# Key pass of a linear attention beside a graph network: exponentials against normalised rows, Wv applied once per layer, turned rows kept in memory

## The chip, the cores and the metric

One core of a Trainium2 chip runs the whole program in one launch. The time is the device time of one execution in microseconds (us); the median of three executions is given, and one further execution was profiled.

## The reference

Per call there are 3125 nodes with 256 features, 100000 edges, and three parts whose results are summed and normalised:

```
xn = layernorm(x)
x  = x + gnn(xn, edge_attr, src, dst) + mix(xn)          # the two parts share nothing but xn
x  = x + moe(layernorm(x))                               # 16 experts, the best 2 for each row

mix, 4 layers, 8 heads of 32:
  h = layernorm(x) * g1 + b1
  q = softmax over each head of (h Wq) * s ; k = softmax over all 3125 rows of (h Wk) * s ; v = h Wv
  context = k^T v (per head) ;  x = x + (q context) Wo + bo
  x = x + gelu((layernorm(x) * g2 + b2) W1 + b1) W2 + b2  # 256 -> 1024 -> 256
gnn: relu([xn[src], attr] W1^T + b) summed by dst, then two products and a row norm
```

All products are in float32. The graph part has no work of a layer in it, and the kernel spreads its edge work over the four layers.

## The kernel before, in words

The 3125 rows are 25 tiles of 125 rows, in 5 groups (g) of 5 tiles. A layer (l) has three stages.

- **Key pass** (lines 1252 to 1285 on PE, 1675 to 1713 on DVE, 977 to 994 on ACT). For each group: keys are made transposed in four units (two of three tiles, two of two tiles; L1259), values in three units (`rows_at`, L1210, from `Wv_s`) that DVE copies to `V5` (L1697). DVE takes the running maximum (L1683) and the shift, ACT makes the exponentials `eT` (L983) and a correction `corr`. PE turns the normalised rows of the next group (`normalised_T`, L1220), ACT applies gain and shift (`features`, L910) into `TT`; PE turns `eT` (L1273), ACT copies it to `es` (L915), PE multiplies `es` with `V5`, 129 columns a head pair (the last column is ones and sums the exponentials; L1283), and DVE adds that to `ctxS` (L1711).
- **Middle** (L1287 to L1307): queries of group 0, the context turned and multiplied with Wo into `M_s` (L1299, L1730), attention of group 0 (`attention`), queries of group 1, the second norm of group 0.
- **Feed-forward pass** (L1310 to L1347), group by group: first product with W1 in 8 blocks f, each of 8 matmuls (L1319, ACT applies Gelu, L1015); then the turned rows and queries of group g+2, `queries_T` and `attention` of group g+1, and the second product of group g (`out_rows`, L1210). Groups 0 to 2 hold queries, groups 0 to 3 hold an attention.

Between these stand 224 edge steps (`step`, `pe_edges`, `act_edges`, `dve_edges`). A step is two bf16 products (L441, after the DMA of `aT`), on DVE `z` = product + gathered rows `G` (L481), on ACT `zr` (L449), on DVE the sum of the step before (L461), the one-hot matrix (L468) and `zl` (L455), and on PE in the next step eight products (L433, L434) that wait for `zl`. The tables `ST_K`, `ST_M`, `ST_P` say how many steps stand in each group: 2 or 3 in a key group, 4 in the middle, 8 or 7 in a feed-forward group.

Every engine runs its own list in the written order; the lists meet in semaphores. PSUM is used as two rings: `RING`, three banks that ACT frees (`ring`: unit u waits until u-3 is free), and `ROW`, two banks that DVE frees (`row_of`). SP issues the DMAs in one list: the `aT` loads, and at a layer's end the weights of the next (`weights_B`, 2.5 MB), which stand ahead of the next layer's first `aT`. GpSimd issues the gathers of `G`.

Of the kernel before, what the change touches and what calls it, by code (L numbers as in the profile page):

```python
# [11 lines left out]
def build(nc, x, src, dst, edge_attr, gnn_W1, gnn_b1, gnn_W2,  # L12
# [8 lines left out]
    T = 125  # L21
# [43 lines left out]
    zn_d = dram("zn_d", (N, D), f32)  # L65
    y_d = [dram(f"y{i}_d", (N + SL, D), f32) for i in range(2)]

    with ExitStack() as ctx:
# [47 lines left out]
        xT_all = over("xT", [128, 2, KD, 128], f32)  # L116
        xT_room = sb("xT_room", [128, 2 * KD * 128])
        QT = sb("QT", [128, KD, GT * T])
        V5 = sb("V5", [T, GT, KD, 129])
# [15 lines left out]
        ctxS = sb("ctxS", [128, KD, 129])  # L135
        ctxN = sb("ctxN", [128, KD, 128])
# [6 lines left out]
        corr = sb("corr", [128, 2, KD])  # L143
# [73 lines left out]
        V_rows = V5[:, :, :, :].rearrange("p j k n -> p (j k n)")[:, 0:GT * D].rearrange("p (j d) -> p j d", d=D)  # L217
# [52 lines left out]
        xs = [sb(f"xs{i}", [128, D])[:, :] for i in range(2)] + [TT[:, i, 0:D] for i in range(2)]  # L270
# [45 lines left out]
        cn_done, rk_done = sem("cn_done"), sem("rk_done")  # L316
# [27 lines left out]
        RING_GA = 4 + LNU + GT  # L344
# [3 lines left out]
        ROW_GA = NRP + 2  # L348
        RING_GP = [2 * NF + (LNU if g + 2 < NG else 0) + (GT + LNU if g + 1 < NG else 0) for g in range(NG)]
        ROW_GP = [NRP * (1 + (g + 1 < NG) + (g + 2 < NG)) for g in range(NG)]  # L350
        RING_MP, ROW_MP = 1 + LNU + GT + LNU, 3 * NRP + KD
        RING_A, RING_L = NT, LNU + NG * RING_GA + RING_MP + sum(RING_GP)
# [10 lines left out]
        HN_L = 3 * NT  # L363
# [4 lines left out]
        ST_K = [[2, 3 - l % 2, 3, 2, 2] for l in range(L)]  # L368
# [5 lines left out]
        def ring_k(l, g):  # L374
            return RING_A + l * RING_L + LNU + g * RING_GA

# [16 lines left out]
        def set_p(g):  # L393
            return 3 + NG + sum(1 + (n + 2 < NG) for n in range(g))

# [3 lines left out]
        def ring_q1(l, g):  # L399
            return ring_h1(l, NG) if g == 0 else ring_k(l, NG) + 1 if g == 1 else ring_p(l, g - 2) + 2 * NF  # L400

        def ring_qT(l, g):
            return ring_k(l, NG) + 1 + LNU if g == 0 else ring_p(l, g - 1) + 2 * NF + (LNU if g + 1 < NG else 0)
# [4 lines left out]
        def row_q(l, g):  # L408
            return row_k(l, NG) if g == 0 else row_k(l, NG) + 2 * NRP + KD if g == 1 else row_p(l, g - 2) + NRP

        def row_ao(l, g):
            return row_k(l, NG) + NRP + KD if g == 0 else row_p(l, g - 1)
# [1574 lines left out]
```

## Time and profile before

| | |
|---|---|
| time, median of 3 runs | 2347.33 us (2338.67, 2347.33, 2349.57) |
| time of the profiled execution | 2337.08 us, of which span 2335.3 us |
| PE busy | 1986.8 us (85%), weight loads 1637.1 us |
| DVE busy | 1520.7 us (65%) |
| ACT busy | 926.8 us (40%) |
| GpSimd busy | 1360.3 us (58%) |
| mean granted TensorE clock | 0.941 |

PE is TensorE, PEld its weight loads, DVE VectorE, ACT ScalarE, SP the engine that issues the DMAs. Busy time is the union of an engine's instructions. A matmul in float32 shows as two instructions, a transpose as one. The mean length of a matmul holds some 0.16 us that overlaps the next one, so the pace of a run of matmuls is read from the starts. In a timeline, an entry in square brackets is the idle time of the engine ahead of the row and what ended it.

### The profile page before, as it was taken

How to read it: one execution, taken by the hardware profiler on the slowest of the kernel's cores; microseconds unless marked ns; L12 is line 12 of the kernel's file. 1: busy time of each engine (PE TensorE's matmuls, PEld its weight loads, DVE VectorE, ACT ScalarE, POOL GpSimd, SP SyncE). 2: the span in 40 equal slices, each digit the busy share in tenths (PEclk: the TensorE clock that was granted, in tenths of full speed). 3: DMA queues.
4: the chain of work that ended last, by engine and by line, in shares of the span. 5: the costliest groups of instructions: out<-in, count | busy, mean ns of one | idle time of the engine just before them, and what ended most of it. 6: DMA issues, size and time to landing. Idle time of an engine off the chain costs nothing. (4 is left out here: it accounts for less than half of the span.)

```text
span 2335.3 us, 33082 instructions
## 1 busy us (share of the span) xinstructions
PE 1986.8 (85%) x10654; PEld 1637.1 (70%) x10654; DVE 1520.7 (65%) x3443; ACT 926.8 (40%) x1948; POOL 1360.3 (58%) x1123
## 2 busy tenths in 40 slices
PE   2449899999888999989899998989999885799990
PEld 1337677778776787877677777767777775788880
DVE  4748877776787777678777766887676457411116
ACT  1224444444445444344544443444444322233330
POOL 4156566677566666756666675656667500466650
PEclk7769999999999999999999999999999976899995
DMA  9553233233332233343232234233223521799997
GB/s 212 174 159 78 67 76 72 71 78 85 105 76 69 71 74 74 83 109 82 65 73 72 71 84 108 69 87 74 71 71 84 124 77 45 238 307 304 304 286 169
DMA packets 269780, 268.49 MB, mean 115 GB/s; under 512 B 146075, under 2 KB 203486, under 8 KB 269630
## 3 DMA queue, kind: packets, MB, share of 16 engines
q0 software_dynamic: 127488, 134.76, 24.2%
q1 hardware_dynamic: 138030, 131.85, 19.2%
q8 instruction: 75, 1.23, 0.2%
q10 hardware_dynamic: 4112, 0.03, 0.1%
q14 instruction: 75, 0.61, 0.1%
HBM read 230.37 MB, written 35.05 MB: 114 GB/s over the span
## 5 line engine op out<-in xcount | busy, mean ns | idle before, releaser
L846 POOL DMA_INDIRECT G<-P_d,src_T x896 | 1138.6, 1271 | 648.0 <-DVE z L481 383.9
L481 DVE TENSOR_TENSOR z<-bank,G 125x512 f32<-125x512 f32 x448 | 288.2, 685 | 167.4 <-PE bank L441 127.8
L1210 PE MATMUL bank<-W_s,hid 128*125 128x256 f32 x1600 | 363.2, 381 | 25.5 <-DVE qe L1621 25.5
L449 ACT ACTIVATE zr<-z 125x512 fp32r<-125x512 f32 x448 | 265.9, 627 | 293.7 <-DVE z L481 292.8
L455 DVE SCALAR_TENSOR_TENSOR zl<-z,zr 125x512 fp32r<-125x512 f32 x448 | 289.8, 688 | 131.1 <-ACT zr L449 131.1
L1319 PE MATMUL bank<-TT,W_s 128*128 128x250 f32 (+1 forms) x1280 | 356.1, 431 | 0.0
L1210 PEld LDWEIGHTS bank<-W_s,hid 128*125 128x125 f32 x1600 | 293.8, 188 | 71.7 <-issue 30.0
L1319 PEld LDWEIGHTS bank<-TT,W_s 128*128 128x128 f32 x1280 | 240.0, 192 | 95.3 <-issue 4.6
L433 PE MATMUL bank<-zr,onehot 125*125 125x256 f32 x896 | 267.6, 331 | 21.7 <-DVE zl L455 21.5
L1015 ACT ACTIVATE hid<-bank,b_s 128x375 f32<-128x375 f32 x320 | 166.1, 520 | 192.5 <-PE bank L1319 184.5
L434 PE MATMUL bank<-zl,onehot 125*125 125x256 f32 x896 | 226.8, 284 | 0.0
L433 PEld LDWEIGHTS bank<-zr,onehot 125*125 125x125 f32 x896 | 169.6, 189 | 46.1 <-DVE onehot L468 16.3
L910 ACT ACTIVATE TT<-bank,lnp 128x375 f32<-128x375 f32 x240 | 127.3, 614 | 143.1 <-PE bank L1220 142.1
L441 PE MATMUL bank<-Wst,aT 128*125 128x512 bf16 x448 | 138.1, 388 | 54.1 <-DMA aT<-attr_d 50.8
L434 PEld LDWEIGHTS bank<-zl,onehot 125*125 125x125 f32 x896 | 170.3, 190 | 5.9
L468 DVE TENSOR_TENSOR onehot<-iota_n,dst_T 125x500 fp32r<-125x500 f32 x224 | 154.2, 688 | 0.0
L1638 DVE TENSOR_TENSOR X<-bank,X 125x512 f32<-125x512 f32 (+1 forms) x120 | 70.6, 600 | 104.0 <-PE bank L1210 103.9
L1220 PE MATMUL bank<-ident,hn 125*128 125x125 f32 x600 | 95.7, 283 | 35.0 <-DVE hn L1561 14.0
L1084 ACT ACTIVATE QT<-bank,b1e 128x128 f32<-128x128 f32 x256 | 73.3, 370 | 98.6 <-PE bank L1435 98.6
L866 POOL DMA_INDIRECT xs<-zn_d,slot_tok x32 | 31.5, 983 | 138.0 <-DVE slot_tok L1915 121.4
L441 PEld LDWEIGHTS bank<-Wst,aT 128*125 128x125 bf16 x448 | 58.3, 138 | 74.1 <-issue 43.3
L1220 PEld LDWEIGHTS bank<-ident,hn 125*128 125x128 f32 x600 | 67.1, 142 | 61.2 <-ACT TT L910 23.9
(313 smaller groups left out, 3071.7 us busy)
## 6 DMA issues: line engine op xcount, KB each, us to landing
W_s<-in_L_ffn_w SPq DMA_DIRECT2D x64, 512.0 KB
hid<-in_L_ffn_w SPq DMA_DIRECT2D x64, 512.0 KB, 3.9
G<-P_d,src_T POOLq DMA_INDIRECT x896, 4.2
W_s<-in_L_mix_W SPq DMA_DIRECT2D x8, 1024.0 KB, 11.0
aT<-attr_d SPq DMA_DIRECT2D x224, 31.2 KB, 2.6
attr_d<-hn SPq DMA_DIRECT2D x12, 246.1 KB, 4.5
X<-in_x SPq DMA_DIRECT2D x5, 560.0 KB
P_d<-es SPq DMA_DIRECT2D x25, 112.0 KB
```

Source lines behind the costliest of these rows:

```text
L433: nc.tensor.matmul(sum_bank[0:T, 0:D], onehot[:, s, i, :], zr[:, s, i // 2, cols], start=i == 0, stop=False)
L434: ins = nc.tensor.matmul(sum_bank[0:T, 0:D], onehot[:, s, i, :], zl[:, i // 2, cols], start=False, stop=i == ST - 1)
L441: nc.tensor.matmul(edge_bank[k][0:ET, :], aT[:, s, :], Wst[:, 2 * k * D:2 * (k + 1) * D], start=True, stop=True).then_inc(e_done, 1)
L449: nc.scalar.activation(zr[:, s, k, :], z[:, k, :], ACT.Relu).then_inc(r_done, 1)
L455: nc.vector.scalar_tensor_tensor(zl[:, k, :], z[:, k, :], 0.0, zr[:, s, k, :].bitcast(f32), ALU.max, ALU.subtract).then_inc(lo_done, 1)
L468: nc.vector.tensor_tensor(onehot[:, s, :, :], iota_n[0:ET, :].unsqueeze(1).to_broadcast([ET, ST, T]), dst_T[:, ds(e * ST, ST)].unsqueeze(2 ...
L481: nc.vector.tensor_tensor(z[:, k, :], edge_bank[k][0:ET, :], G[:, ST * s + 2 * k:ST * s + 2 * k + 2, :].rearrange("p j d -> p (j d)"), ALU ...
L846: pool.indirect_dma_start(G[:, j, :], None, P_d[:, :], bass.IndirectOffsetOnAxis(ap=src_T[:, at:at + 1], axis=0)).then_inc(g_in[j], 16)
L1015: act.activation(hid[:, f, a * T:b * T], RING[(u - RING_A) % 3][:, 0:(b - a) * T], ACT.Gelu, bias=b1_s[:, l * NF + f:l * NF + f + 1]).then ...
L1210: ins = pe.matmul(to[0:T, (j - a) * D:(j - a) * D + D], w, m, start=n == 0, stop=n == len(pairs) - 1)
L1220: ins = pe.transpose(to[:, (j - a) * T:(j - a) * T + T], hn[:, j, 128 * k:128 * k + 128], ident[0:T, 0:T])
L1319: ins = pe.matmul(to[:, 0:(b - a) * T], W1_s[:, k, part], TT[:, k, TT_PIECES[pc]], start=k == 0, stop=k == KD - 1)
```

## The change

Five things are done, all in the layers.

1. The value product leaves the key pass. The exponentials are multiplied with the **normalised rows** (256 columns, without gain and shift), and the context becomes a 256x256 sum `ctxS`; the sum of exponentials comes from ACT's `accum_out` into `piece_sum` and is kept in `key_sum`. Once per layer `ctxS` is divided by `key_sum` (`ctxN`), turned (4 transposes), given gain and shift (`ctxF`), and multiplied with Wv (4 products, `ctxT`), and then with Wo.
2. This product (`context(g-1)`) is made **one group late**, between the third and the fourth key unit of group g; that of group 4 stands at the head of the middle. Rows and turned rows alternate between two buffers (`hn`/`hn2`, `TT`/`TTQ`).
3. The turned rows of each group are **kept in memory**: SP writes them to `nT_d` after the key pass's `features` (641 KB a group) and reads them back into `TTQ` for the queries, so the second turning of each group's first norm is gone.
4. Queries of groups 2, 3 and 4 are made **inside the first product** of the feed-forward of group g = 1, 2, 3 (`QIN`, after blocks 1, 3 and 5), for g+1, not for g+2 as before; ACT's exponential stands after block 6.
5. Edge steps are dealt out anew: `ST_K`, `FF_STEP` (steps after blocks 0, 2, 4, 6 in place of 0, 2, 5 and one behind the product); a third step of a key group stands behind the keys; a step stands in the middle of each attention; the first step of a key group's last two stands ahead of `normalised_T`.

```diff
-        ST_K = [[2, 3 - l % 2, 3, 2, 2] for l in range(L)]
+        ST_K = [[2 + l % 2, 2, 2, 2, 3] for l in range(L)]
-        FF_STEP = {0: 0, 2: 1, 5: 2}
+        FF_STEP, FF_Q = {0: 0, 2: 1, 4: 2, 6: 3}, {1: 0, 3: 1, 5: 2}
 # SP
+            def keep_normalised_T(l, g):
+                if g == 0:
+                    sp.wait_ge(nT_in, l * NG * 16)
+                sp.wait_ge(ring_act, ring_h1(l, g) + LNU + 1)
+                sp.dma_start(nT_d[g], NORM_T[g % 2][:, :, :].rearrange("p k n -> p (k n)")).then_inc(nT_out, 16)
+            def load_normalised_T(g):
+                sp.dma_start(TTQ_flat, nT_d[g]).then_inc(nT_in, 16)
             for l in range(L):
+                keep_normalised_T(l, 0)
+                at = step_k(l, 0) + (PG if l == 0 else 0)
+                for g in range(NG):
+                    attr_steps(at, step_k(l, g + 1))
+                    ...
 # ACT, key pass
                             act.activation(eT[:, h, a * T:b * T], RING[(u0 + 2 * pc + h - RING_A) % 3][:, 0:(b - a) * T], ACT.Exp,
-                                           bias=nb[:, pc, h:h + 1], scale=SCALE).then_inc(ring_act, 1)
+                                           bias=nb[:, pc, h:h + 1], scale=SCALE,
+                                           accum_out=piece_sum[:, g % 2, pc, h:h + 1]).then_inc(ring_act, 1)
-                        if pc == 0 and ST_K[l][g] == 3:
-                            step(step_k(l, g))
-                    first_norm(u0 + 4, u0 + 4 - RING_A)
+                    if ST_K[l][g] == 3:
+                        step(step_k(l, g))
+                    if g + 1 < NG:
+                        act.wait_ge(nT_out, (l * NG + g) * 16)
+                        first_norm(u0 + 4, u0 + 4 - RING_A, to=NORM_T[(g + 1) % 2])
 # ACT, middle
+                act.wait_ge(ring_full, uM + 1)
+                for k in range(KD):
+                    ins = act.activation(ctxF[:, k, :], ...)
+                ins.then_inc(ring_act, 1)
                 q_softmax(0)
-                copy_tile(uM, uM - RING_A, ctxT[:, :, :], 128)
-                first_norm(ring_q1(l, 1), ring_q1(l, 1) - RING_A)
                 step(eM)
                 queries_T(0)
 # ACT, feed-forward
                         if f - 1 in FF_STEP:
                             step(e0 + FF_STEP[f - 1])
+                        if QIN[g] and f == 6:
+                            q_softmax(g + 1)
 # PE, key pass
+                def context(g):
+                    r0, uT = row_k(l, g), ring_k(l, g + 1) - GT
+                    for pc, (a, b) in enumerate(PC):
+                        to = row_of(r0 + pc)
+                        for h in range(KD):
+                            for j in range(a, b):
+                                ...
+                                ins = pe.matmul(to[:, D * h:D * h + D], es[:, j, 128 * h:128 * h + 128], NORM[g % 2][:, j, :],
+                                                start=j == a, stop=j == b - 1)
+                        ins.then_inc(row_full, 1)
                     for pc, (a, b) in enumerate(PC):
                         for h in range(KD):
+                            if pc == 1 and h == 1 and g:
+                                context(g - 1)
                             to = ring(u0 + 2 * pc + h)
                             ...
-                        for i in ((0, 1), (2,))[pc]:
-                            rows_at(r0, i, lambda j: [(TT[:, k, tt_cols(j)], Wv_s[:, k, :]) for k in range(KD)])
-                    normalised_T(l * SETS + g + 1, u0 + 4)
+                    if ST_K[l][g] == 3:
+                        step(step_k(l, g))
                     step(step_k(l, g + 1) - 2)
+                    if g + 1 < NG:
+                        normalised_T(l * SETS + g + 1, u0 + 4, NORM[(g + 1) % 2])
 # PE, middle
+                context(NG - 1)
+                queries(0, (0, 1))
                 pe.wait_ge(cn_done, l + 2)
+                ... 4 transposes of ctxN
+                queries(0, (2,))
+                pe.wait_ge(ring_act, uM + 2)
+                ... 4 products of Wv_s with ctxF
+                step(eM)
+                ... products with Wo_s, queries_T(0)
+                attention(0, (0, 1)); step(eM + 1); attention(0, (2,)); queries(1, (0,))
+                step(eM + 2); queries(1, (1, 2)); normalised_T(l * SETS + NG, ring_h2(l, 0), hn); step(eM + 3)
 # PE, feed-forward, behind block f of the first product
                         if f in FF_STEP:
                             step(e0 + FF_STEP[f])
-                    if g + 2 < NG:
-                        normalised_T(l * SETS + set_q1(g + 2), ring_q1(l, g + 2))
-                    step(e0 + 3)
+                        if QIN[g] and f in FF_Q:
+                            queries(g + 1, (FF_Q[f],))
                     if g + 1 < NG:
                         queries_T(g + 1)
-                        attention(g + 1)
-                        if g + 2 < NG:
-                            queries(g + 2, (0,))
+                        attention(g + 1, (0, 1))
                         step(e0 + 4)
-                        if g + 2 < NG:
-                            queries(g + 2, (1, 2))
+                        attention(g + 1, (2,))
 # DVE, key pass: context(g - 1) stands ahead of the maximum of the fourth unit; behind the fourth:
+                    if g + 1 < NG:
+                        normalised(g + 1, NORM[(g + 1) % 2])
+                    if ST_K[l][g] == 3:
+                        step(step_k(l, g))
+                    step(step_k(l, g + 1) - 2)
 # DVE, middle: context(NG - 1), key_sum, ctxN, queries(0), ctxT, q_softmax(0), M_s, step(eM), attention(0, eM + 1), ...
 # DVE, feed-forward
-                    step(e0)
-                    if g + 2 < NG:
-                        dve.wait_ge(ring_full, ring_h2(l, g) + LNU)
-                        normalised(g + 2)
-                    for i in range(1, 4):
+                    for i in range(4):
                         step(e0 + i)
+                        if QIN[g] and i < NRP:
+                            queries(g + 1, (i,))
+                        if QIN[g] and i == NRP - 1:
+                            q_softmax(g + 1)
```

## Rows read from the trace of the kernel before

**Rows 1.** Windows of layer 0: length; busy PE, PEld, DVE, ACT, POOL; clock; DMA; GB/s.
```profile
165.08:254.34 89.26, 82.28 (x483) 68.97 (x481) 77.56 (x190) 44.21 (x101) 61.04 (x49) 1.00 0.30 74
254.34:294.07 39.73, 30.56 (x159) 23.90 (x158) 33.27 (x71) 15.93 (x27) 20.58 (x17) 0.96 0.29 71
294.07:359.03 64.96, 60.87 (x301) 48.66 (x300) 48.25 (x93) 29.34 (x53) 43.65 (x35) 0.97 0.31 75
359.03:420.86 61.83, 58.91 (x302) 47.85 (x300) 45.76 (x98) 28.20 (x52) 40.64 (x33) 1.00 0.30 72
482.68:536.81 54.13, 53.21 (x271) 43.08 (x270) 38.51 (x84) 24.66 (x46) 41.94 (x33) 1.00 0.35 83
```

**Rows 2.** PE in order of time, a key group of layer 0: start, length.
```profile
222.46 2.68 PE L1259 MATMUL bank<-TT,Wk_s 128*128 128x375 f32 x8
224.98 2.75 PE L1210 MATMUL bank<-Wv_s,TT 128*125 128x256 f32 x12
...
232.50 0.60 PE L441 MATMUL bank<-Wst,aT 128*125 128x512 bf16 x2
...
233.88 0.82 PE L1273 MATMUL bank<-ident,eT 128*125 128x128 f32 x6
...
237.28 2.40 PE L1283 MATMUL bank<-V,es 125*128 125x129 f32 x20
239.52 2.69 PE L1259 MATMUL bank<-TT,Wk_s 128*128 128x375 f32 x8
```

**Rows 3.** DVE in order of time in the same key group.
```profile
223.98 1.87 DVE L1561 TENSOR_SCALAR hn<-X,mvA,rstd_t 125x256 f32<-125x256 f32 x5
...
232.97 1.29 DVE L481 TENSOR_TENSOR z<-bank,G 125x512 f32<-125x512 f32 x2 [1.10 <-PE bank L441]
...
236.44 1.29 DVE L481 TENSOR_TENSOR z<-bank,G 125x512 f32<-125x512 f32 x2
```

**Rows 4.** ACT in order of time in the same key group.
```profile
231.51 2.12 ACT L910 ACTIVATE TT<-bank,lnp 128x375 f32<-128x375 f32 x4
233.70 1.23 ACT L449 ACTIVATE zr<-z 125x512 fp32r<-125x512 f32 x2
```

**Rows 5.** PE in order of time, feed-forward of group 1, layer 0.
```profile
368.13 6.47 PE L1319 MATMUL bank<-TT,W_s 128*128 128x375 f32 x24
...
380.05 1.71 PE L1220 MATMUL bank<-ident,hn 125*128 125x125 f32 x10
...
397.31 3.69 PE L1210 MATMUL bank<-W_s,hid 128*125 128x256 f32 x16 [2.11 <-DVE qe L1621]
```

**Rows 6.** ACT in order of time around the same feed-forward group.
```profile
358.81 1.28 ACT L1015 ACT_TABLE_LOAD   x1
360.49 0.57 ACT L1015 ACTIVATE hid<-bank,b_s 128x375 f32<-128x375 f32 x1 [0.40 <-PE bank L1319]
...
398.52 1.27 ACT L962 ACTIVATE qe<-qe 125x1280 f32<-125x1280 f32 x1 [2.31 <-DVE qe L1621]
```

**Rows 7.** DVE in order of time, the rest of the queries' softmax.
```profile
415.30 1.47 DVE L1627 TENSOR_REDUCE qs<-qe 125x40 f32<-125x1280 f32 x1
...
418.66 1.28 DVE L481 TENSOR_TENSOR z<-bank,G 125x512 f32<-125x512 f32 x2
```

**Rows 8.** Windows as in rows 1: layer 0's middle, layer 1's start, two key passes.
```profile
270.30:273.70 3.40, 0.78 (x7) 0.56 (x7) 3.33 (x5) 0.00 (x0) 2.21 (x2) 1.00 0.38 91
273.80:277.10 3.30, 3.30 (x14) 2.83 (x13) 3.11 (x7) 3.10 (x8) 1.76 (x2) 0.50 0.16 42
...
583.00:596.00 13.00, 9.92 (x46) 7.43 (x44) 8.63 (x32) 4.18 (x10) 2.42 (x2) 1.00 0.84 239
...
582.67:674.42 91.75, 81.45 (x473) 67.64 (x472) 74.13 (x191) 43.45 (x99) 51.05 (x42) 1.00 0.35 91
1002.63:1097.71 95.08, 84.36 (x482) 70.35 (x481) 77.22 (x197) 44.83 (x101) 56.20 (x46) 0.98 0.36 93
```

**Rows 9.** PE in order of time, first edge step of layer 1.
```profile
596.19 0.65 PE L441 MATMUL bank<-Wst,aT 128*125 128x512 bf16 x2 [2.45 <-DMA aT<-attr_d]
```

More of the change, by code:

```diff
@@ L343, in build @@
         LNU = 2 * KD
-        RING_GA = 4 + LNU + GT
+        RING_GA = [4 + (LNU if g + 1 < NG else 0) + GT for g in range(NG)]
         RP = ((0, 2), (2, 3), (3, 5))
@@ L901, in std, with features @@
                 act.activation(to, var, ACT.Sqrt, bias=epsc[0:T, :]).then_inc(s, 1)
-            def features(u, loc, gain, shift):
+            def features(u, loc, gain, shift, to=TT):
                 for pc, (a, b) in enumerate(PC):
@@ L1211, in rows_at, with normalised_T @@
                 ins.then_inc(row_full, 1)
-            def normalised_T(n, u):
+            def normalised_T(n, u, rows):
                 for pc, (a, b) in enumerate(PC):
@@ L1240, in bias_row, with attention @@
                     return onesb[:, 0:T], brow[:, l * D:(l + 1) * D]
-                def attention(g):
-                    for i in range(NRP):
+                def attention(g, units):
+                    for i in units:
                         pe.wait_ge(ring_act, ring_qT(l, g) + RP[i][1] + 1)
@@ L1304, in _ @@
-                queries(1)
+                attention(0, (0, 1))
+                step(eM + 1)
+                attention(0, (2,))
+                queries(1, (0,))
                 step(eM + 2)
-                normalised_T(l * SETS + set_h2(0), ring_h2(l, 0))
+                queries(1, (1, 2))
+                normalised_T(l * SETS + NG, ring_h2(l, 0), hn)
                 step(eM + 3)
@@ L1643, in row_stats, with attention, second_norm @@
                         dve.bn_stats(st[:, j, :], tile(X, g * GT + j)).then_inc(s_stat, 1)
[L1645 removed]
+                def attention(g, middle):
                     r = row_ao(l, g)
[L1647 to L1651 removed]
+                    residual(g, r, 0)
+                    residual(g, r, 1)
+                    row_stats(g, r, 0, st5b, b_stat)
+                    step(middle)
+                    residual(g, r, 2)
+                    row_stats(g, r, 1, st5b, b_stat)
+                    row_stats(g, r, 2, st5b, b_stat)
                     aggregate(b_stat, b_aggr, l * NT + g * GT, st5b, mv5b)
[L1654 removed]
+                def second_norm(g, free=None):
                     n = l * NG + g + 1
@@ L1735, in _ @@
-                second_norm(0, ring_q1(l, 1) + LNU)
+                    dve.tensor_tensor(M_s[:, h, :], ROW[(r - ROW_A) % 2][:, 0:D], bo8[:, l * D:(l + 1) * D], ALU.add).then_inc(row_dve, 1)
+                step(eM)
+                attention(0, eM + 1)
+                queries(1, (0,))
+                second_norm(0)
                 step(eM + 2)
+                queries(1, (1, 2))
+                step(eM + 3)
                 q_softmax(1)
-                step(eM + 3)
                 for g in range(NG):
```

248 lines of the change are left out of this document (118 added, 130 removed).

## The prediction

> **What bounds the kernel now.** I read the busy time by stage first [rows 1]. In layer 0 the key pass up to the last group's context product (89.3 us) keeps PE busy for 82.3, the middle (39.7) for 30.6, a feed-forward group with queries (61.8) for 58.9, one with an attention and no queries (54.1) for 53.2. The reader is to see two things. PE is the bound of the feed-forward groups and nearly that of the key pass; but DVE is busy for 77.6 of the key pass's 89.3, so there the second engine has little more room than the first. Then the order in time: a key group of two edge steps takes 17.06 us from key product to key product, all PE work but 0.9 [rows 2], and DVE's and ACT's lists for the same group are as full [rows 3, 4]. In the feed-forward group the one large hole is 2.11 us before `out_rows`, where PE waits for DVE to take the queries from their bank [rows 5]. So an instruction taken from PE helps only where the chain through DVE and ACT isn't as long as what is left on PE. That is the question in every step below.
>
> **PE work.** Per key group the value product goes: 12 matmuls in 2.6 us and 8 more at that pace, 4.3 us [rows 2]. The context product grows from 129 to 256 columns: 20 matmuls took 2.24 us (237.28 to 239.52) and will take 20 x 0.215 = 4.3, so +2.1. Twenty sets of ten transposes go, one of them in each feed-forward group with queries, 1.55 us there (380.05 to the next step, its overlap of 0.16 taken off) [rows 5]. Once per layer two transposes and four products come, some 1.1. Over four layers that is -86 + 42 - 30 + 4 = -70 us, and with the 12 holes of 2.11 us, -95. This is what the change would give if PE alone set the time.
>
> **Key group.** After the change PE has 16.2 - 4.3 + 2.1 = 14.0 us in 17.06. I walk the chain that is left, t = 0 at the first key product. Three key units take until 3.4 (two of 1.26 [rows 2], one at 250 columns 0.85), the late context product until 7.7, the fourth unit until 8.5. Only now can DVE take the last maximum and make the shift (0.4, and three tiny operations of 0.2 each) and reach 9.8; normalised rows of the next group, 1.87 [rows 3], until 11.8. They stood at the head of the group before and are now behind the fourth unit. From there two lines run: the last turned rows reach ACT at 12.1, whose four `features` (2.12 [rows 4]) began at 11.4 and end at 13.6; DVE's `z` of the step ends at 13.0. ACT does `zr` (1.2) until 14.8, then the copies of the turned exponentials; PE can turn the fourth and fifth tile only when the first two copies have freed their banks, at 15.7 (three banks), and makes the last step, 1.38 (232.50 to 233.88 [rows 2]), until 17.1. DVE is not behind: its last step is 3.47 long (232.97 to 236.44 [rows 3]) and is done at 2.5 of the next group, before the context rows come. So the group takes 17.1, as before: 3.1 us of PE work become idle time. Bounds: 14.0 (PE alone) and 18.8 (the clock, below). I take 17.1.
> A group with three steps now has the third ahead of the other two with nothing between: the second waits for the first's `zl`. With `features` to make it comes to 20.4 (the same walk, +3.5 of DVE's step, less 0.2 that it overlaps); the last group, which has none, to 17.6.
> First group of a layer: no late context; 14.4 in layer 0. In layers 1 to 3 the first `aT` lies behind 2.6 MB of weights and lands 13.5 us after the layer's start (596.19 against 582.67), and PE waited 2.45 for it [rows 9], since 4.3 us of values and the transposes stood ahead of the step. That cover is gone: PE reaches the step at 7. And the save of `nT` (0.64 MB) is now issued ahead of `aT`; at 239 GB/s [rows 8] it takes 2.7 us, so `aT` lands at 16.2. The rest of the group behind it takes 7.1 with two steps (23.3), 10.1 with three (26.3).
> Sum of a key pass up to the context product of group 4: layer 0 14.4 + 3 x 17.1 + 17.6 = 83.3 against 89.3; layer 2 23.3 + 51.3 + 17.6 = 92.2 against 95.1; layers 1 and 3 26.3 + 51.3 + 17.6 = 95.2 against 91.8 and about the same [rows 1, 8]. In all -6.0 - 2.9 + 3.4 + 3.4 = -2.
>
> **Feed-forward groups with queries (1, 2, 3; twelve in all).** A block f takes PE 2.1 us (three in 6.31 [rows 5]). Queries between the blocks wait for nothing, so the 1.55 of transposes and the 2.11 go, and 0.4 of small waits (61.83 - 58.91 in rows 1 holds them all): -4.1. But the softmax has lost its lead. ACT may start it only behind Gelu of block 6: a table load of 1.28, the exponential 1.27 [rows 6], then DVE 3.36 (415.30 to 418.66 [rows 7]). That ends 6.6 us after block 6 leaves PE (0.6 for the last Gelu included). PE has a step and block 7, 3.5 us, so `queries_T` starts 3.3 us late (with semaphores). DVE does the fourth edge step behind the softmax; ACT does that step's `zr` ahead of the query copies; so after three transposes PE waits again for a bank, 1.3. Together +4.6, against -4.1: +0.5, and 0.3 of that goes in rounding of the pieces; 61.9 without the clock. Bounds of this wait: 3.3 (if the copies come at once) and 6.3.
>
> **Middle and group 0.** Walking it in the same way from the start of the late context product: queries 0 and the turned context are hidden, but `q_softmax(0)` ends at 15.7, PE having run out at 12.6, and the copies of turned queries wait for a `zr` that stands ahead of them until 18.6. With the rest 35.8 against 39.7. Feed-forward group 0 loses its queries and transposes: 54.1 as group 3 did, and 2.8 for DVE, which comes late with `q_softmax(1)` and the step ahead of it: 56.9 against 65.0. Group 3 in turn gets queries: 61.9 against 54.1.
>
> **The clock.** PE's granted clock was 1.00 in the key and feed-forward stretches. In the middle of layer 0 PE was busy for 0.78 of 3.4 us, and in the 3.3 us after it the clock was 0.50, the 1.2 GHz level, with PE busy throughout [rows 8]: 1.7 us lost. The first wait for `aT` (2.45 us idle) was followed by full clock. The new wait of 3.3 and 1.3 us around three transposes leaves PE as idle as the middle, so I price a fall behind each of the twelve, about half of it covered by the waiting: +0.8 each; +1.3 in the middle and +1.2 in group 0; +1 in each of the three waits for `aT`. In steady key groups PE is idle for about half of the 6 us before its last step, in pieces of 1.3 us and less; I leave the clock at full there but for a few: +3 in all.
> The page "TensorE: Matmul & The Clock Gate" of the Trainium skill (section "HAM oscillation — how this bites in real kernels") speaks against this change: gaps on PE cost a second time, because what follows them runs at half clock. By that rule the gaps that the removed work leaves in key groups would be paid too; rows 8 bear it out for the deep gap only.
>
> **Sum.** Key passes -2 + 3 + 3 = +4. Per layer: middle 37.1 and group 0 58.1 against 104.7 (-9.5), groups 1 and 2 62.7 against 61.8 (+1.8), group 3 62.7 against 54.1 (+8.6): +0.9, four times +3.6. In all +7.6 us, on the profiled execution's own time of 2337.1 (span 2335.3 and 1.8 around it): 2345. That execution was 10.3 under the median of the runs shown, 2347.3; on the median's scale I say 2354. It is a change of 0.3%, and less than 0.5% (12 us) can't be told from none here.
>
> **Rivals.**
> *PE alone is the bound.* Then -95 at most, 2252. For it: PE's 85% and the 99% of group 3. Against it: the walk of the key group. 5%.
> *Half of it comes through* because the chain in the key group is shorter than my walk by 2 us (14 to 16 groups): -30, 2325. For it: many of my hand-overs could overlap. 17%.
> *Slower: the clock falls in key groups too.* Place: each steady key group, between `normalised_T` and the last step. Price: half clock in what follows, 1.7 us, on the chain, 16 groups: +27, so 2381. Against it: the pieces of idle time are shorter than those of the middle. From 7 such groups on it makes the change a loss of over 0.5%. 18%.
> *The query wait is longer.* ACT's table is loaded at a price of 1.28 with nothing behind it in rows 6: the load ends at 360.09, and Gelu starts at 360.49 after a wait for PE. If the switch of tables needed another 1.4 us of draining, each of twelve would be +1.4: +17, 2371. 4%.
> The page "ScalarE: Activation LUTs" of the Trainium skill (section "What ACT_TABLE_LOAD costs") puts a drain of about 1.38 us on top of the load. By that rule this last rival is right; rows 6 leave at most 0.4 for it.
>
> **How the numbers follow.** Forecast 56%, of which nearly all is within 0.5%, with some 16 of the 56 beyond it above (its own range 2338 to 2370). Rivals as above, 5 + 17 + 18 + 4. Faster by over 0.5%: 5 + 15 and 3 for errors elsewhere, with 2 of the forecast: 25%. Slower: 18 + 4 + 16: 38%. Within: 37%. The range takes in the half gain and the slow clock: 2314 to 2384.
>
> **What would show it.** Key groups of two steps 17 us apart with some 3 us of PE idle before the last transposes and the last step; 14 to 15 would prove me wrong. `queries_T` (L1236) waiting 3 us for DVE's softmax in groups 1 to 3, groups of 62 to 63. The first `aT` of layers 1 to 3 waited for by 8 us or more. A clock under 1.00 in feed-forward groups. I am wrong if the DMA saves delay gathers so that `z` waits for `G`, which I cost at nothing because SP's and GpSimd's queues together use 0.30 of the DMA engines in these stretches [rows 1]; it would cost the landing time of a save, 2.7 us, for each that collides.

## The result, and the profile after

The changed kernel takes 2386.7 us (median of 4 runs, 2382.7 to 2387.9) against 2348.5 for the kernel before on the same chip: ratio 1.0168, 95% interval 1.0136 to 1.0200. It is slower by 1.7%. The forecast was 2354 with a range up to 2384, "no change".

Page of the kernel after: span, PE's share, clock and, of the costliest groups, the edge steps' first product.
```profile
span 2383.8 us, 31958 instructions
PE 1975.7 (83%) x10094; PEld 1616.7 (68%) x10094; DVE 1474.3 (62%) x3371; ACT 913.3 (38%) x1964; POOL 1351.9 (57%) x1123
PEclk9769999999899999989999999999999976899995
L436 PE MATMUL bank<-Wst,aT 128*125 128x512 bf16 x448 | 143.1, 399 | 76.2 <-DMA aT<-attr_d 66.9
```
PE lost 560 instructions but only 11 us of busy time (1986.8 before), because more of what is left ran at half clock: the mean granted clock fell from 0.941 to 0.921. As an estimate, 0.059 of 2335 us and 0.079 of 2384 us are 138 and 188 us of full-clock time lost, 50 more than before; most of that is PE busy at half speed, so the work taken away comes to somewhat under 60 us, of the 70 forecast. PE idled 76.2 us ahead of L436, against 54.1 before.

Windows of the kernel after, columns as in [rows 1]: layer 0's key pass, its middle, feed-forward groups 1 and 3, then layers 1 and 2 whole.
```profile
162.67:248.82 86.15, 75.06 (x362) 58.01 (x361) 67.56 (x179) 42.34 (x115) 52.95 (x43) 0.96 0.42 109
248.82:288.89 40.07, 31.32 (x158) 25.93 (x157) 31.00 (x69) 12.44 (x23) 22.15 (x18) 0.91 0.39 104
346.17:410.82 64.65, 60.01 (x291) 48.86 (x290) 44.09 (x91) 27.86 (x48) 40.51 (x33) 0.95 0.32 79
475.57:538.68 63.11, 58.48 (x291) 47.87 (x290) 44.10 (x91) 27.86 (x48) 39.70 (x33) 0.97 0.29 70
...
585.34:1024.04 438.70, 391.04 (x1893) 315.04 (x1892) 308.16 (x677) 186.91 (x366) 276.96 (x221) 0.94 0.36 91
1024.04:1457.56 433.52, 387.57 (x1884) 312.32 (x1882) 304.10 (x671) 185.87 (x364) 273.06 (x217) 0.95 0.36 91
```
Against [rows 1], feed-forward group 1 carries 11 PE instructions fewer and 1.1 us more PE busy time (60.01 against 58.91), at a clock of 0.95 against 1.00. I split both spans at the first key product of each group and sum over the four layers, against the terms of the forecast:

| stretch | forecast | measured |
|---|---|---|
| ahead of layer 0 | 0 | -2.4 |
| key passes | +4 | +12.3 |
| middle and group 0 | -38 | +2.0 - 29.6 = -27.6 |
| groups 1 and 2 | +7.2 | +21.7 |
| group 3 | +34.4 | +39.4 |
| group 4, and what follows the layers | 0 | +5.1 |
| sum | +7.6 | +48.5 |

The 48.5 us compare the two profiled executions, so 41 us were missed. On the medians it is 38 us of change and 33 missed, because the profiled execution before lay 10 us under its median.

**The query wait and the clock behind it.** PE in order of time in feed-forward group 1 of layer 0, kernel after:
```profile
369.35 0.59 PE L436 MATMUL bank<-Wst,aT 128*125 128x512 bf16 x2
...
370.72 2.27 PE L1362 MATMUL bank<-TT,W_s 128*128 128x375 f32 x8
376.14 0.86 PE L1265 MATMUL bank<-ident,qe 125*128 125x125 f32 x6 [3.14 <-DVE qe L1670]
378.27 1.09 PE L1265 MATMUL bank<-ident,qe 125*128 125x125 f32 x4 [1.27 <-ACT QT L941]
379.15 5.25 PE L1239 MATMUL bank<-M_s,QT 128*125 128x256 f32 x12
```
ACT and then DVE in the same time:
```profile
370.04 1.28 ACT L988 ACT_TABLE_LOAD   x1
371.33 1.27 ACT L988 ACTIVATE qe<-qe 125x1280 f32<-125x1280 f32 x1
...
376.71 1.23 ACT L444 ACTIVATE zr<-z 125x512 fp32r<-125x512 f32 x2 [1.87 <-DVE z L476]
377.85 0.90 ACT L941 ACTIVATE QT<-bank 128x250 f32<-128x250 f32 x3
```
```profile
374.59 1.49 DVE L1670 TENSOR_TENSOR qe<-qe,qr 125x1280 f32<-125x1280 f32 x1
376.00 1.28 DVE L476 TENSOR_TENSOR z<-bank,G 125x512 f32<-125x512 f32 x2
```
The two waits came out at 3.14 and 1.27 us where 3.3 and 1.3 stood. The last PE row matters most: 12 attention products take 5.25 us, where 12 products of the same shape take 2.75 elsewhere. Windows over this place:
```profile
374.40:377.50 3.10, 0.86 (x6) 0.63 (x6) 3.07 (x5) 1.23 (x4) 0.52 (x1) 0.98 0.00 0
377.50:384.30 6.80, 6.03 (x17) 4.81 (x18) 2.59 (x5) 2.01 (x6) 4.50 (x4) 0.51 0.28 63
```
The clock is at the 1.2 GHz level for 6.8 us, of which PE is busy for 6.03: some 3 us lost. The forecast had half as long a fall, half of it covered, and 0.8. Ten of the twelve groups show this fall and took 64.2 to 64.8 us; the other two (group 3 of layers 0 and 3) show one of 3.4 us and took 63.1.

**Key group.** PE in order of time, steady group of layer 0 (212.93 to 229.84, 16.91 us):
```profile
212.93 3.53 PE L1302 MATMUL bank<-TTQ,Wk_s 128*128 128x375 f32 x12
216.29 4.48 PE L1289 MATMUL bank<-hn,es 125*128 125x256 f32 x20
220.61 1.01 PE L1302 MATMUL bank<-TTQ,Wk_s 128*128 128x250 f32 x4
...
223.34 1.53 PE L1249 MATMUL bank<-ident,hn 125*128 125x125 f32 x8 [0.35 <-DVE hn L1600]
...
227.89 0.73 PE L1315 MATMUL bank<-ident,eT 128*125 128x128 f32 x4 [0.85 <-ACT es L941]
```
17.1 was forecast.

**First group of layer 1**, PE:
```profile
590.82 1.11 PE L1302 MATMUL bank<-TT,Wk_s 128*128 128x250 f32 x4 [1.96 <-ACT eT L1009]
600.21 1.11 PE L436 MATMUL bank<-Wst,aT 128*125 128x512 bf16 x2 [8.28 <-DMA aT<-attr_d]
```
The load came 14.9 us after the layer's start (585.34) and PE waited 8.28 for it, against 2.45 in [rows 9], where it came 13.5 us after the start. What follows took 13.0 us and not 10.1: its first product ran at half clock too (1.11 for what takes 0.59 at full clock).

**Gathers.** GpSimd, then DVE, at the end of layer 0's key pass and the head of its middle (248.82):
```profile
246.14 1.62 POOL L872 DMA_INDIRECT G<-P_d,src_T  x1 [0.31 <-issue]
248.06 1.21 POOL L872 DMA_INDIRECT G<-P_d,src_T  x1 [0.30 <-issue]
249.58 1.21 POOL L872 DMA_INDIRECT G<-P_d,src_T  x1 [0.31 <-issue]
```
```profile
243.87 1.29 DVE L476 TENSOR_TENSOR z<-bank,G 125x512 f32<-125x512 f32 x2
...
250.82 0.69 DVE L476 TENSOR_TENSOR z<-bank,G 125x512 f32<-125x512 f32 x1 [2.21 <-DMA G<-P_d,src_T]
```
A step needs four gathers, 1.5 us apart, so 6 us of GpSimd. The last key group now makes its three steps 3.4 and 4.1 us apart (`z` at 240.43, 243.87, 247.92), and the gathers fall behind: from 242.93 on GpSimd issues one after the other with 0.3 us between them. Over the whole span DVE waits for `G` 20 times, 37.8 us, against 3 times and 11.6 us before; 16 of the 20 stand at the head of a middle or in feed-forward group 0, where the kernel before has none.

### The profile page after: what moved, and what is told of

Same layout as the page of the kernel before. It is cut to its first block, busy times and chain, and to the rows that moved or that the text cites. A ratio compares the mean times of both kernels' runs of the same rounds, so it can differ in the third digit from the quotient of the medians.

```text
span 2383.8 us, 31958 instructions
## 1 busy us (share of the span) xinstructions
PE 1975.7 (83%) x10094; PEld 1616.7 (68%) x10094; DVE 1474.3 (62%) x3371; ACT 913.3 (38%) x1964; POOL 1351.9 (57%) x1123
## 3 DMA queue, kind: packets, MB, share of 16 engines
q1 hardware_dynamic: 143790, 157.50, 22.1%
## 4 chain that ended last, share of the span: by engine, by line
PE 59%; DVE 14%; DMA 9%; ACT 7%; issue 4%; POOL 3%; SPq 2%; DVEq 1%; POOLq 0%; ACTq 0%
PE bank L1239 24%; PE bank L1362 12%; PE bank L428 3%; PE bank L429 3%; DMA TTQ<-zn_d,slot_tok 3%; PE bank L436 3%; PE bank L1289 3%; PE bank L1474 2%; PE bank L1302 2%; PE bank L1482 2%; ACT zr L444 2%; DMA aT<-attr_d 2%; DVE z L476 2%; DMA G<-P_d,src_T 1%; POOL G L872 1%
## 5 line engine op out<-in xcount | busy, mean ns | idle before, releaser
L1362 PEld LDWEIGHTS bank<-TT,W_s 128*128 128x128 f32 x1280 | 234.7, 189 | 92.0
L428 PE MATMUL bank<-zr,onehot 125*125 125x256 f32 x896 | 272.8, 336 | 20.4 <-DVE zl L450 20.4
L436 PE MATMUL bank<-Wst,aT 128*125 128x512 bf16 x448 | 143.1, 399 | 76.2 <-DMA aT<-attr_d 66.9
L436 PEld LDWEIGHTS bank<-Wst,aT 128*125 128x125 bf16 x448 | 62.0, 145 | 101.3 <-issue 52.1
L1239 PE MATMUL bank<-M_s,QT 128*125 128x256 f32 x400 | 127.7, 482 | 0.0
L936 ACT ACTIVATE TT<-bank,lnp 128x250 f32<-128x250 f32 (+1 forms) x128 | 67.8, 610 | 118.0 <-PE bank L1249 118.0
L1239 PEld LDWEIGHTS bank<-M_s,QT 128*125 128x125 f32 x400 | 96.4, 250 | 19.0
L892 POOL DMA_INDIRECT TTQ<-zn_d,slot_tok x32 | 31.4, 982 | 136.3 <-DVE slot_tok L1956 119.7
```

The source lines that it names most:

```text
L428: nc.tensor.matmul(sum_bank[0:T, 0:D], onehot[:, s, i, :], zr[:, s, i // 2, cols], start=i == 0, stop=False)
L436: nc.tensor.matmul(edge_bank[k][0:ET, :], aT[:, s, :], Wst[:, 2 * k * D:2 * (k + 1) * D], start=True, stop=True).then_inc(e_done, 1)
L1239: ins = pe.matmul(to[0:T, (j - a) * D:(j - a) * D + D], w, m, start=n == 0, stop=n == len(pairs) - 1)
L1362: ins = pe.matmul(to[:, 0:(b - a) * T], W1_s[:, k, part], TT[:, k, TT_PIECES[pc]], start=k == 0, stop=k == KD - 1)
```

## The experiments

The kernel before, timed in the same three sets of runs: 2347.9 (x1 to x4), 2347.8 (x5 to x8) and 2346.7 (x9 to x12). The ratios are to these; "gained" is against the 2386.7 of the kernel after, which was timed beside 2348.5. "Groups" are those of the feed-forward pass, if not called key groups.

**x1_lead.** Queries at blocks 0, 1, 2, softmax behind block 4 instead of 6, on DVE ahead of the edge steps 2 and 3.
```
-        FF_STEP, FF_Q = {...}, {1: 0, 3: 1, 5: 2}
+        FF_STEP, FF_Q = {...}, {0: 0, 1: 1, 2: 2}
-                        if QIN[g] and f == 6:      # ACT: q_softmax
+                        if QIN[g] and f == 4:
```


> The changed kernel with queries made behind blocks 0, 1 and 2 of the first product and their exponential behind block 4 (not behind 1, 3, 5 and 6). Theory A (the loss of the change is the softmax that ends after the product does, and the half clock that its idle time brings): groups 1 to 3 of the feed-forward fall from 64.6 us to 58 (PE's work alone), queries_T waits for nothing, the clock stays at 1.00 there; twelve groups, -75 us, about 2310. Theory B (the exponential inside the product costs by itself, because two table loads stop Gelu and the ring of three banks fills): the 3 us of waiting move to block 5 or 6, groups at 62 or more, -30 us at most, 2357. Theory C (the loss is in the key pass and the middle): under 10 us of change, 2377 or more.

2375.7 us, ratio 1.0119 (1.0080 to 1.0159): 11 us gained, not 75 and less than the 30 that theory B allowed. PE's waits in group 1 of this kernel:
```profile
369.49 0.94 PE L436 MATMUL bank<-Wst,aT 128*125 128x512 bf16 x2 [1.18 <-DVE z L476]
...
371.61 0.35 PE L428 MATMUL bank<-zr,onehot 125*125 125x256 f32 x1 [1.18 <-DVE zl L450]
...
378.47 0.70 PE L1265 MATMUL bank<-ident,qe 125*128 125x125 f32 x4 [0.88 <-ACT QT L941]
```
The wait for the softmax is gone, and the edge steps inside the product now wait for DVE, which makes the softmax (3.4 us) ahead of their `z`. Groups of 63.8, 62.1 and 63.8: the wait moved, as theory B has it, and in each group 1 and 3 the clock still fell for 3.4 us.

**x2_at_first.** In layers 1 to 3 the two first loads of `aT` are issued ahead of `weights_B` and the save of `nT`.
```
-                at = step_k(l, 0) + (PG if l == 0 else 0)
+                at = step_k(l, 0) + PG
```


> The changed kernel with the first two aT loads of layers 1 to 3 issued ahead of the next layer's weights and of the saved rows. If the wait for aT is the cost of the first key groups of layers 1 to 3 (27.9, 25.5 and 26.9 us; 16.1 in layer 0): they fall to 16 with two steps and 19 to 20 with three, -26 us in all with the clock, 2361. Rival (what waits there is DVE's work left from the layer before, or gathers slowed by the weights): less than 8 us of change, 2379 or more.

2361.1, ratio 1.0056 (1.0038 to 1.0074). First key groups of 20.6, 14.8 and 22.1 us, against 27.9, 25.5 and 26.9 after: 22.8 of the 25.6 us gained, as expected.

**x9_before_at.** The same edit on the kernel before, as a control.
```
-                attr_steps(step_k(l, 0) + (PG if l == 0 else 0), ...)
+                attr_steps(step_k(l, 0) + PG, ...)
```


> The kernel before, with the two first loads of turned rows of layers 1 to 3 issued ahead of the feed-forward weights, as in x2_at_first. A control: theory A (the change took away what PE did ahead of its first edge step, so the load's landing costs much more after than before): PE waited 2.45 us for it before, three layers, so the time falls by 5 to 9 us only, to about 2340, against the 26 of x2_at_first. Rival B (the load is late by its own place in SP's queue and costs the same in both kernels): the fall is 20 us or more.

2339.1, ratio 0.9962 (0.9943 to 0.9982): 7.6 gained. The load was late in both kernels: it came 13.3 to 13.6 us after the layer's start before, and 14.9 to 15.0 after, where the save stands ahead of it. PE's wait for it grew by 5.8 to 6.2 us a layer. Of that, 1.4 to 1.7 is the later landing; the larger part is that the change removed what PE did in the meantime (values and transposes). The lateness costs three times as much.

**x3_copies.** ACT copies the turned queries ahead of the `zr` of the step that stood before them, in the middle and in groups 1 to 3.
```
                 q_softmax(0)
-                step(eM)
                 queries_T(0)
+                step(eM)
...
                         queries_T(g + 1)
+                        if QIN[g]:
+                            step(e0 + 3)
```


> The changed kernel with ACT's copies of the turned queries ahead of the edge step's zr, in the middle and in feed-forward groups 1 to 3. If the second wait (1.3 us in groups 1 to 3, 2.1 in the middle) counts as it stands in the trace: groups 63.0 to 63.4, middle 38, -25 us with the clock, 2362. Rival (the step's zr is then late and PE waits for zl in the step that follows, or the clock eats the same time anyway): under 8 us of change.

2350.5, ratio 1.0011 (0.9994 to 1.0029): 36 gained, against the 25 of the expectation. Its profiled execution was the fastest of its ten, 2336.1, so the stretches below sum to more than 36. PE in group 1:
```profile
365.74 2.27 PE L1364 MATMUL bank<-TT,W_s 128*128 128x375 f32 x8
371.15 1.61 PE L1267 MATMUL bank<-ident,qe 125*128 125x125 f32 x10 [3.15 <-DVE qe L1672]
372.60 2.75 PE L1241 MATMUL bank<-M_s,QT 128*125 128x256 f32 x12
```
The wait of 3.15 us for DVE is untouched, the second wait is gone, and the 12 products behind take 2.75 us. This group took 60.57 us, but it is the only one of the twelve without a fall of the clock. Group 2, and the window behind its wait of 3.15:
```profile
401.75:463.48 61.73, 58.36 (x291) 48.09 (x290) 44.22 (x91) 28.02 (x48) 39.92 (x33) 0.97 0.33 82
431.50:434.80 3.30, 3.08 (x13) 2.84 (x14) 2.29 (x5) 2.22 (x6) 1.93 (x2) 0.50 0.07 8
```
Ten groups show a fall of 3.4 us and took 61.6 to 62.3, one (group 2 of layer 3) a fall of 6.8 and took 63.2. So the one long wait brings a fall too; taking the second away halves its length. A fall of 3.4 us cost 1.0 to 1.7 us a group and not the 0.8 of the forecast. The middles, 40.1 to 40.7 before this edit, took 35.6 to 37.0: a saving of 16.6 over four layers.

**x6_fill.** The wait stays, but PE is kept busy: 14 products into a free bank, unused.
```
                 def queries_T(g):
+                    if g >= 2:
+                        to = ring(ring_qT(l, g))
+                        for i in range(14):
+                            pe.matmul(to[0:T, :], onesb[:, 0:T], Wst[:, 0:2 * D], ...)
                     pe.wait_ge(q_norm, l * NG + g + 1)
```


> The kernel after, with 14 added products of 125 x 512 into the free bank of the ring, issued on PE ahead of the wait for q_norm in queries_T of groups 2 and 3 and of group 1 in no layer (g >= 2 alone); their results are not used. The wait itself stays. Theory A (the idle stretch ahead of the attention products is what lets the clock fall, and the fall costs 2.5 to 3 us): granted clock 1.00 through queries_T and the 12 attention products of groups 1 and 2, these groups 64.6 -> about 62.3, 8 groups in all, the time falls by 16 to 20 us to about 2368. Rival B (the groups are long because DVE stands on their path, and PE's clock is beside the point): the groups stay at 64 to 65 and the time within 5 us of 2386.7, or above it by what the added products take.

2353.8, ratio 1.0026 (1.0008 to 1.0044): 33 gained by adding work, theory A's cause and nearly twice its size. It acts in groups 1, 2 and 3 (twelve, not the eight of the expectation). PE, and the window of group 1:
```profile
370.98 3.19 PE L1264 MATMUL bank<-Wst,onesb 128*125 128x512 bf16 x14
374.29 0.86 PE L1269 MATMUL bank<-ident,qe 125*128 125x125 f32 x6
376.42 0.70 PE L1269 MATMUL bank<-ident,qe 125*128 125x125 f32 x4 [1.27 <-ACT QT L941]
376.96 2.75 PE L1239 MATMUL bank<-M_s,QT 128*125 128x256 f32 x12
```
```profile
340.33:402.14 61.81, 60.19 (x305) 48.68 (x305) 44.10 (x92) 27.75 (x48) 40.54 (x33) 1.00 0.34 83
```
The second wait is as before (1.27) and the clock is full. All twelve groups took 61.8: that is the walk of the prediction without its clock (61.9). The groups took 30.1 us less together than in the kernel after: the fall cost 2.5 us a group.

**x4_all3.** The edits of x1, x2 and x3 together.

> The three edits of the runs before in one. If they are separate costs: with the lead the copies edit counts only in the middle (-8), so -75 - 26 - 8, 2278, faster than the kernel before (2348) by 3%. If they share one cause (DVE's list as a whole is the bound), less than the largest of the three alone plus 10 us.

2340.7, ratio 0.9960 (0.9937 to 0.9983). 46 gained, of the 109 that separate costs would give. Groups of 62.6 to 63.9, worse than 60.6 to 63.2 with the copies alone: an earlier softmax pushes DVE's edge steps into PE's way (x1), and adds nothing once the copies stand first. The first key groups took 20.6, 14.8 and 20.6, as in x2.

**x5_undo.** The queries back in their old place: those of g+2 behind the product of group g, three steps inside it; turned rows still from memory, context product still late.
```
-                        if QIN[g] and f in FF_Q:
-                            queries(g + 1, (FF_Q[f],))
+                    step(e0 + 3)
...
+                        if g + 2 < NG:
+                            queries(g + 2, (1, 2))
```


> The kernel after, with the queries of group g+2 again issued behind the products of group g, three edge steps inside the first product (at parts 0, 2 and 5), one behind it and the softmax of g+2 at the group's end; the turned rows still come from memory and the late context products stay. Theory A (the feed-forward's order is what was lost: the fall of the clock behind the wait for qe, plus the softmax on DVE inside the group): groups 0 to 2 take 60.3 us (61.83 of before less the 1.55 of its transposes), group 3 takes 54.1, the granted clock is 1.00 through queries_T, and the time falls by 50 to 60 us, to about 2327 to 2337. Rival B (the rows' way through memory is what costs, by SP's queue and the DMA engines): the groups stay above 62.5 and the time falls by less than 25, to above 2362.

2347.5, ratio 0.9984 (0.9966 to 1.0001): 39 gained, between the two theories (50 to 60, or under 25). Groups 1 and 2 took 60.2, or 61.9 where the clock fell for 3.4 us, group 3 54.1, group 4 45.8, as expected; group 0 took 65.1 to 65.5, as before, and that is what the expectation left out: with its queries back it costs 7.8 more than in the kernel after. Per layer 287.2 (65.1 + 60.2 + 61.9 + 54.1 + 45.8, layer 0) against 296.4 (57.3 + 64.7 + 64.8 + 63.1 + 46.7). The first key groups of layers 1 to 3 stayed at 25.8 to 29.4 us. The turned rows still go through memory here, so that way isn't what made groups 1 to 3 long.

**x8_undo_at_cop.** x5 with the loads of x2 and, in the middle, the copies of x3.

> The kernel of x5_undo, with the two first loads of turned rows of layers 1 to 3 issued ahead of the feed-forward weights and of the row save (as in x2_at_first) and ACT's copies of turned queries ahead of the edge step in the middle (as in x3_copies). Theory A (three causes on different stretches of the layer add up): -60 - 26 - 8 to -16, about 2285 to 2295, under both kernels. Rival B (they share a cover, as the three of x4_all3 did, which gave 46 where 109 stood): about 2310 to 2325.

2311.3, ratio 0.9838 (0.9817 to 0.9860). The total lies where rival B had it (2310 to 2325), not theory A (2285 to 2295). But the two edits took another 36 off x5, as theory A had for them (34 to 42): on different stretches they add up, and the total misses theory A mainly by what x5 missed.

**x11_acf.** The kernel after with the loads of x2, the copies of x3 and the added products of x6.

> The kernel after with three edits: the loads of x2_at_first, the copies of x3_copies and the 14 added products of x6_fill. Theory A (two shares of the queries' cost in the feed-forward groups, a wait and a clock): the added products keep the clock at 1.00, the groups go from 60.6 to 62.3 in x3_copies to 60.3 to 60.8, another 1 us each, and the first key groups save 26: 2350 - 26 - 12 = about 2312. Rival B (with the copies early, the idle time is already too short to lose the clock but rarely, so that the added products only stand in PE's way): groups of 61.8 as in x6_fill, about 2325.

2307.8, ratio 0.9822 (0.9791 to 0.9854): the lowest median here, 79 us under the change as it was and 39 under the kernel before, and theory A's figure (2312) rather than rival B's (2325). Window of group 1:
```profile
345.80:406.37 60.57, 60.18 (x306) 48.70 (x305) 43.95 (x91) 27.65 (x48) 40.30 (x33) 1.00 0.33 84
```
All twelve groups take 60.6, PE is busy for 60.18 of 60.57, and 3.19 us of that are the added products.

**x7_ctx129.** The late context product 129 columns wide; the kernel leaves out the right 127 columns of each half, so its output is wrong in part.
```
-    pe.matmul(to[:, D*h:D*h + D], es[...], NORM[g % 2][:, j, :], ...)
+    pe.matmul(to[:, D*h:D*h + 129], es[...], NORM[g % 2][:, j, 0:129], ...)
```


> The kernel after, with the key pass's context products 129 columns wide instead of 256 (full width in the first group alone); the right 127 columns of each half then hold old values, so the output is wrong in part. Theory A (PE's own work and what waits for it set the key group: a walk over both gave 17.1 us for the group): 18 key products' columns less is 18 x 0.053 us = 1 us off PE's chain, and each group falls from 16.9 to about 16, the time by 10 to 20 us. Rival B (DVE's two edge steps and its part of the context set the group, and PE waits for them): the groups stay at 16.9 and the time within 5 us of 2386.7.

2372.3, ratio 1.0090 (1.0070 to 1.0111). The product took 2.23 us at its pace (201.90 to 204.13) instead of 4.3, and steady key groups took 15.1 to 15.5 instead of 16.9:
```profile
201.90 2.40 PE L1290 MATMUL bank<-hn,es 125*128 125x129 f32 x20
204.13 1.01 PE L1303 MATMUL bank<-TT,Wk_s 128*128 128x250 f32 x4
...
207.13 1.53 PE L1249 MATMUL bank<-ident,hn 125*128 125x125 f32 x8 [0.57 <-DVE hn L1601]
```
So, as theory A has it, the key group hangs on PE's late product, nearly one for one (1.4 to 1.8 of 2.1 us). The expectation undersized the cut: 127 of 256 columns in 20 products is 2.1 us, not 1.

**x10_behind.** The late context product behind the fourth key unit.
```
-                            if pc == 1 and h == 1 and g:
-                                context(g - 1)
...
+                    if g:
+                        context(g - 1)
```


> The kernel after, with the late context product of a key group issued behind the fourth key unit instead of ahead of it, on PE and on DVE. Theory A (the fourth unit behind the product is what makes the last key group 18.9 us instead of the 17.6 priced and 14.8 of before: the last exponentials and so the last turned tiles come 4.3 us later): the last group falls to 17 to 17.5, the others from 16.9 to about 16.4 since the normalised rows start 0.5 us sooner; 4 x 1.6 + 12 x 0.5 = 12 us, to about 2374. Rival B (the edge steps' chain through z, zr and zl sets the group, wherever the product stands): the groups stay within 0.2 us and the time within 5 us of 2386.7.

2427.7, ratio 1.0341 (1.0310 to 1.0373): 41 slower, against both theories. PE in this kernel:
```profile
217.41 3.53 PE L1300 MATMUL bank<-TTQ,Wk_s 128*128 128x375 f32 x12
222.29 1.11 PE L1300 MATMUL bank<-TTQ,Wk_s 128*128 128x250 f32 x4 [1.35 <-ACT eT L1009]
223.24 4.48 PE L1289 MATMUL bank<-hn,es 125*128 125x256 f32 x20
```
The fourth unit needs a bank of `RING`, and that comes free only when ACT has made the first exponentials, which wait for DVE's maximum and the step ahead of it. The late product had filled this time. Now PE waits 1.35 us for it, and the product starts 5.8 us after the group's start instead of 3.4. This key group takes 19.5 us for 16.9; the 1.35 come through to the transposes, and its last edge step, from 234.32 on, runs at half clock (2.6 us for 1.4). The other key groups behind the first take 18.3 to 20.6 us, but the second groups of layers 1 to 3 23.5 to 23.8.

**x12_uac_behind.** The same edit on x8.

> The kernel of x8_undo_at_cop with the late context product behind the fourth key unit, as in x10_behind. Theory A: the key groups fall as in x10_behind, 12 us, to about 2299. Rival B: within 5 us of 2311.

2354.0, ratio 1.0019 (0.9996 to 1.0043): 43 slower than x8, again against both theories, and the same loss on another base.

## Why the prediction was wrong, point by point

- **PE work, key group, query wait**: right in length. 16.91 for 17.1; waits of 3.14 and 1.27 for 3.3 and 1.3; without the clock the feed-forward group takes 61.8 (x6) for 61.9. PE work removed became waiting, as forecast, and "PE alone" (2252) was never near. But the sign "3 us of PE idle" in a key group did not come: PE was busy for 15.33 of 16.91 us. Some 1 us of the missing 1.5 is in transposes paced by others, eight in 1.53 us and six in 1.35, where eight take 1.02 at full clock in the middle and six took 0.82 in [rows 2]. Two slips of the working move nothing: PE was busy for 98% of group 3, not 99%, and 61.83 + 0.5 - 0.3 is 62.0, not 61.9.
- **The clock** is the step that failed: "so I price a fall behind each of the twelve, about half of it covered by the waiting: +0.8 each". [Rows 8] showed one fall of 3.3 us, and I took its length for all. In ten of the twelve groups it lasted 6.8 us, with PE busy in nearly all of it. x6 puts it at 2.5 a group: 20 us of the 41 missed. The rule of the Trainium skill that I weighed ("TensorE: Matmul & The Clock Gate", section "HAM oscillation — how this bites in real kernels"), that a gap costs a second time by what runs slowly behind it, is borne out here at full price. The trace before already has one fall of 6.8 us, in the middle of layer 3, and the forecast left it out:

```profile
1533.20:1536.60 3.40, 2.82 (x10) 2.23 (x10) 3.33 (x4) 0.00 (x0) 2.56 (x3) 0.51 0.39 93
1536.70:1540.10 3.40, 3.14 (x13) 2.90 (x14) 3.10 (x7) 2.28 (x6) 1.21 (x2) 0.50 0.21 61
```

- **Middle**: 37.1 priced, 40.1 to 40.7 measured, +12 to +13. The wait for the softmax (3.17 us in layer 0) and the one behind `zr` (1.93) came, but the softmax ended 17.6 us after the start and not 15.7: DVE stood 2.21 us for `G` at the head, a term costed at nothing. Behind it the clock fell for 6.8 us again (from 268.1 in layer 0). x3 takes the second wait and most of the fall away, with the softmax as late as before (17.5), and the middle falls to 35.6 to 37.0. Layer 0 of x3 tells the two terms apart: it keeps the late softmax, has full clock and took 35.6; of the 4.4 less, 1.9 are the second wait and 2.5 the clock, priced at 1.3. So about 1.2 of the 3 us are the clock and 1.9 the late softmax.
- **Group 0**: 58.1 priced, 57.3 measured in three layers, 58.1 in the fourth: right.
- **First key groups of layers 1 to 3**: landing forecast at 16.2, measured 14.9; but 27.9, 25.5 and 26.9 for 26.3, 23.3 and 26.3. The rest behind the load ran largely at half clock (window of layer 1's first group from 602.5: 0.68). Priced at +1 each, what follows the load took 2.9, 3.4 and 1.8 us more than the walk. The place was right: x2 and x9.
- **Last key groups**: 17.6 priced, 18.9 to 19.0 measured. DVE's part behind the fourth unit ended at 9.95 us, near the 9.8 of the walk, but its first `z` began only at 10.6, after 0.64 us for which the profile names no cause, and three steps then follow one another through DVE. The clock fell here too, for 3.4 us from 244.3 on in layer 0: ten transposes took 2.81 us, where six and four took 1.35 and 0.73 in the group before. The other misses of the key passes are smaller and were not followed: 16.1 for 14.4 in the first group of layer 0, and 19.1 and 18.9 for 17.1 in the second groups of layers 1 and 3, each with a fall of the clock.
- **Group 4 of the feed-forward**: 46.65 for 45.86, a stretch costed at nothing. With the queries in their old place (x5, x8) it is 45.8 again, so it comes with the new order of steps; which edit of it isn't shown.
- **Rivals.** The half gain (2325) needed key groups 2 us shorter than the walk; they were 0.2 shorter. The clock in key groups (2381) came nearest in time but not in place: steady key groups stayed at full clock and 16.91, and only first, second and last groups of a pass show falls. The draining of ACT's table is refuted: the load starts at 370.04, lasts 1.28, and the exponential starts at 371.33, 0.01 us later. The 1.38 us that the Trainium skill puts on top ("ScalarE: Activation LUTs", section "What ACT_TABLE_LOAD costs") aren't there, while the load itself agrees.
- **Gathers at nothing**: wrong. I had named the mechanism (`z` waits for `G`) but looked for it in the DMA queues; it came from steps that stand closer together than GpSimd can issue their gathers. Against the DMA queues stands the landing of a gather around the head of layer 0's middle, 4.2 us in the median before and after alike. The cost is read from rows only: at the heads of the four middles `z` waited 2.21 to 3.45 us for `G`, and PE then 1.32 to 2.57 for `ctxS`, where 0.8 to 0.9 were waited for it before; it is part of the late softmax. In group 0 twelve waits of 16.7 us together left the stretch within its price of 58.1. No run spread the steps, so the mechanism isn't tested.

## What to carry to other kernels

Work removed from the bounding engine pays only where the chain through the others is shorter; elsewhere it becomes idle time, and on TensorE idle time can be charged again in the clock. Before pricing a wait, price the fall of the clock behind it too, and look at whether a second, short wait stands close behind the first. Reordering ACT so that the second wait goes (x3, 1.3 us in a group and 1.7 to 1.9 in a middle) gave 36 us, and filling 3.2 us with useless products (x6) gave 33 with no wait of the others shortened, while moving the softmax forward (x1) gave 11. And ask of every removed instruction what was late behind it: here a load (x2, x9), and in the key pass the late product itself was the cover of a bank's wait (x10).

## What the runs showed of the hardware

One idle time of 3.15 us ahead of the attention (x3, twelve places) was followed by half clock for 3.4 us in ten places, for 6.8 in one and by full clock in one. The same idle time with 0.86 us of transposes and a second wait of 1.27 behind it (the kernel after, twelve places) was followed by half clock for 6.8 us in ten places and for 3.4 in two. A fall of 6.8 us cost 2.3 to 2.9 us of a group's time, one of 3.4 cost 1.0 to 1.7. Products of 125 x 512 in bf16 whose result nobody reads, at 0.23 us each, kept the clock at 1.00 in all twelve groups of x6, through the second wait of 1.27 too, and in all twelve of x11. Twelve products of 256 columns took 2.75 us at the 2.4 GHz level and 5.25 at 1.2.
